# A wide Toeplitz table loaded in eight bands of 16 partitions in place of four bands of 32

## What is computed

```python
# layer 0: linear attention over the normalised image, then a layer norm
x = x + _L0_conv_ref(_gn(x), L0_conv_w_qkv, ...)
# layer 1: 7 x 7 depthwise circular convolutions, by FFT in the reference
gate_A = sigmoid(conv(x, gate_A_kernel)); gate_B = sigmoid(conv(x, gate_B_kernel))
b_t = conv(x, B_kernel) * gate_B
# 8 equal steps of a gated scan, then h_final @ W_out + b_out
x = x + _L1_conv_ref(_gn(x), ...)
```

## Time and profile before

| | before |
|---|---|
| median of 3 runs | 6455.65 us (6454.68 to 6463.24) |
| the profiled execution | 6477.81 us, span 6476.0 us |
| busy: TensorE matmul, weight load | 87%, 80% |
| busy: VectorE, ScalarE, GpSimd | 66%, 61%, 65% |
| moved by DMA | 1440.33 MB, mean 222 GB/s |
| granted TensorE clock, mean | 0.953 |

### The profile page before, as it was taken

How to read it: one execution, slowest core, us unless ns; L and a number is a source line. 1 busy time by engine, 2 the same in 40 slices (tenths; PEclk the granted TensorE clock), 3 DMA queues, 4 the chain that set the end, 5 groups by cost and what they waited for, 6 DMA issues and landing times. The chain is left out here.

```text
span 6476.0 us, 143235 instructions
## 1 busy us (share of the span) xinstructions
PE 5612.8 (87%) x51252; PEld 5161.6 (80%) x51252; DVE 4301.7 (66%) x5123; ACT 3942.8 (61%) x5128; POOL 4179.6 (65%) x3608
## 2 busy tenths in 40 slices
PE   6789999999999999999972688888888888888887
PEld 5578888888888888888862578887878778888887
DVE  6367667776667676677745976666666667666653
ACT  5677677776677666677522456565555555565554
POOL 0146666666666666676674977767667677677651
PEclk9899999999999999999986799999999999999999
DMA  5457777777777777777664599999999999999987
GB/s 129 130 158 224 218 221 224 224 218 217 219 222 221 222 218 218 217 226 222 183 175 131 150 252 257 266 260 261 254 251 256 251 260 262 254 266 260 251 239 211
DMA packets 1239217, 1440.33 MB, mean 222 GB/s; under 512 B 142960, under 2 KB 1025396, under 8 KB 1238516
## 3 DMA queue, kind: packets, MB, share of 16 engines
q1 hardware_dynamic: 1238516, 1431.07, 77.8%
HBM read 999.09 MB, written 431.64 MB: 221 GB/s over the span
## 5 line engine op out<-in xcount | busy, mean ns | idle before, releaser
L1231 PE MATMUL psC<-wide,xhl 128*128 128x256 bf16 x6144 | 1058.0, 283 | 58.1 <-DMA wide<-toeplitz_wide 47.3
L1228 PE MATMUL psC<-wide,xhl 128*128 128x192 bf16 x6144 | 877.6, 253 | 0.0
L1161 POOL TENSOR_TENSOR stage<-stage,nrow 128x1024 f32<-128x1024 f32 x240 | 622.4, 2593 | 365.6 <-DMA stage<-x_by_block_row 354.4
L787 POOL TENSOR_TENSOR y<-y,grow 128x1024 f32<-128x1024 f32 x256 | 606.1, 2367 | 344.1 <-DVE y L654 344.1
L1178 POOL COPY down<-xhl 48x448 f32<-48x448 f32 x512 | 505.8, 988 | 490.9 <-PE psC L1237 387.2
L1322 ACT ACTIVATE xhl<-psC 128x512 f32<-128x512 f32 x512 | 303.3, 599 | 694.5 <-PE psC L1237 693.0
L1237 PE MATMUL psC<-narrow,down 128*128 128x96 bf16 x6144 | 540.3, 213 | 162.2 <-POOL down L1181 95.8
L1228 PEld LDWEIGHTS psC<-wide,xhl 128*128 128x128 bf16 x6144 | 646.8, 116 | 20.2
L1231 PEld LDWEIGHTS psC<-wide,xhl 128*128 128x128 bf16 x6144 | 598.3, 116 | 73.5 <-DMA wide<-toeplitz_wide 47.1
L1429 DVE SCALAR_TENSOR_TENSOR xhl<-xhl,psC 128x512 f32<-128x512 f32 x512 | 346.6, 680 | 466.6 <-ACT xhl L1322 466.1
L1337 ACT ACTIVATE hT<-psH 128x512 f32<-128x512 f32 x512 | 304.8, 595 | 539.3 <-PE psH L1273 539.0
(11 more groups left out here) (167 smaller groups left out, 13803.6 us busy)
## 6 DMA issues: line engine op xcount, KB each, us to landing
wide<-toeplitz_wide SPq DMA_DIRECT2D x1024, 140.0 KB, 5.8
xa<-in_x SPq DMA_DIRECT2D x256, 512.0 KB, 4.5
xb<-in_x SPq DMA_DIRECT2D x256, 512.0 KB, 3.6
xc<-in_x SPq DMA_DIRECT2D x256, 512.0 KB, 5.8
x_rows<-xc SPq DMA_DIRECT2D x256, 512.0 KB
res<-x_rows SPq DMA_DIRECT2D x256, 512.0 KB, 8.7
out<-res SPq DMA_DIRECT2D x256, 512.0 KB, 8.0
stage<-x_by_block_row SPq DMA_DIRECT2D x225, 512.0 KB, 8.4
```

Of the source, the lines that this page charges most:

```text
L787: nc.gpsimd.tensor_tensor(y[:], y[:], grow[:].unsqueeze(1).to_broadcast([P, TPC, C]), ALU.mult).then_inc(s_yg, 1)
L1161: nc.gpsimd.tensor_tensor(v, v, nrow[:, 0:1, :].to_broadcast([P, NP_, C]), ALU.mult).then_inc(s_scaled, 1)
L1228: nc.tensor.matmul(dst[:, :, :, 2:], lhs, tab[:, :, 32 + part * 12:44 + part * 12], start=False, stop=False)
L1231: nc.tensor.matmul(dst, lhs, tab[:, :, part * 16:part * 16 + 16], start=(n == 0), stop=False)
```

## The change

A second list of ranges, `LOADS`, has eight bands for groups of 16 partitions: rows 0 to 2, 0 to 4, 0 to 6, 0 to 8, 2 to 10, 4 to 12, 6 to 14 and 8 to 16. `load_wide` issues eight DMAs by it in place of four, and TensorE's wait counts 16 for each of them. Setup goes on storing by `BANDS`. Ring depths and the order of everything else stay.

```diff
 BANDS = [(max(0, 4 * g - 6), 4 * g + 4) for g in range(4)]
+LOADS = [(max(0, 2 * g - 6), 2 * g + 2) for g in range(8)]
...
-                for g in (0, 2, 1, 3):
-                    lo, hi = BANDS[g]
-                    rows = slice(g * 32, (g + 1) * 32)
+                for g in (0, 4, 2, 6, 1, 5, 3, 7):
+                    lo, hi = LOADS[g]
+                    rows = slice(g * 16, (g + 1) * 16)
                     sp.dma_start(wide[rows, blk % WR, lo:hi].rearrange("p r c e -> p (r c e)"),
                                  wide_d[blk, rows, lo * CB * WCOL:hi * CB * WCOL]).then_inc(s_w[blk % WR], 16)
...
-                pe.wait_ge(s_w[k], img * (64 * uses(NBLK, WR, k)) + 64 * (blk // WR + 1))
+                pe.wait_ge(s_w[k], img * (16 * len(LOADS) * uses(NBLK, WR, k)) + 16 * len(LOADS) * (blk // WR + 1))
```

## The result

The changed kernel takes 6976.95 us (median of 4 runs, 6969.61 to 6987.72), the kernel before beside it 6459.44 us (6454.68 to 6470.68). The ratio is 1.0804, 95% interval 1.0782 to 1.0826: slower by 8%, 517 us. The forecast was slower by 2.5%, 6615 us, and at most 6790. The profiled execution took 6987.72 us, its span 6985.9.

A forecast was written before the change was run, and what follows sets the result against it. The SP queue issuing every DMA was to become the bound: 14 images x (9.1 + 2.5) = 162 us on 6477.8 or the 6455.65 median, giving 6640 or 6618; forecast 6615 us, +2.5%, range 6420 to 6790.

The forecast's parts named there:

- 128 x 0.466 = 59.6 us per image: SP queue, second layer: four more wide-load DMAs per block, 128 per image, each priced at 0.466 us.
- The slot of 0.466 us: SP queue: one wide load's price, its median issue of 0.421 us plus a gap of 0.045 us.
- the high end of the slot (0.53 us): SP queue: estimated upper average price of one wide load with stalls in it, 67.8 us per image.
- at least 4.1: End of an image, SP already full: blocks spaced 3.47 us between narrow loads go to at least 4.1 us.
- a twentieth of the old waits: SP queue, steady images: 2.5 us per image added for imperfect packing, out of 50.5 us of waits.
- I take nothing for the bytes: Wide table, 84 KB less per block: possible gain of 0 to 7.9 us per image, counted as nothing.
- Faster by shorter issues: SP's wide loop: issues of 0.35 us leave SP waits, lighter DMA cuts table waits; 6400 or 6345 us; chance 0.17.
- DMA engines: Wide-table transfers: 16 partitions may be written more slowly; at half of today's rate 6800 us; chance 0.12.
- threshold of 11.9 GB/s: Wide table per DMA engine: 364 KB fit the remaining 1.96 us per block only above this rate, 70% of 17.0.
- SP's waits for blocks: Sign on the SP queue: waits for finished blocks fall from 599 us to under a tenth of the period.
- the median issue: Sign on the SP queue: a wide load's median issue time stays at 0.42 us.
- the image at 188 us: Sign in the second layer: the steady image takes about 188 us, against 176.8 us before.

The follow-up runs named there:

- the run made for it: Kernel before with its four wide loads covering 16 partitions and all 16 rows each, same bytes and number of issues: 6783.96 us, ratio 1.0492.

## Why the prediction was wrong, point by point

**The mechanism was right; SP's added work was priced too low.** That SP becomes the bound is shown three ways: it waits 0.7 us per image for blocks; the time moves by at most 0.5% with the bytes (1.0804, 1.0789 and 1.0751 with 364, 448 and 56 KB); and it goes with the number of its issues, 6459 us at four, 6977 at eight, 7895 at twelve. The step that failed is "128 x 0.466 = 59.6 us per image": it adds slots at their median and leaves all other issues at their old price. The added work measured 84.6 us.

**The account.** Per image SP went from 126.3 to 210.9 us of work, where 185.9 was forecast, and from 50.5 to 0.7 us of waits, where I allowed 2.5. The pieces:

- The slot of 0.466 us, times 128: 59.6 us. Right; the median issue is 420 ns, eight in a row take 3.65 us, and from eight issues to twelve the image grows by 60.1 us.
- The narrow load's median issue went from 0.320 to 0.522 us, 32 x 0.202 = 6.5 us. I had left it at its old price. The row of before that could have warned me is the narrow load at 4432.44, issued in 0.52 us right behind a store. In the kernel before its median is 0.52 us within 0.15 us behind a store or a stage load and 0.32 us when the queue had paused for over 0.7 us; right behind a wide load it is 0.35 us (0.36 in the changed kernel). So 0.32 us was the price behind a pause, and the changed queue has hardly any.
- The issues of over 1 us rose from 10.3 to 30.0 us per image above the medians of their kinds: 19.7 us. I had seen them and put them in the high end of the slot (0.53 us) but not in the forecast. Neither value was the right form: they are no part of an added wide load's price, since twelve issues have no more of them than eight. They come where the queue loses its pauses, above all behind stores and residual loads. At the end of an image I even left them out of a row that showed them: the 3.47 us between two narrow loads hold 1.2 us of them, and with four more slots make 5.3 us, not "at least 4.1"; in the changed kernel they follow each other after 5.5 us at the median where only wide loads stand between.
- Together 59.6 + 6.5 + 19.7 = 85.8 us, 1.2 us more than the 84.6 measured; that rest is not assigned.
- The waits left, 0.7 in place of 2.5 us: 1.8 us too many. I had taken a twentieth of the old waits, a number with no row behind it. SP never caught up except a few times.

6.5 + 19.7 - 1.2 - 1.8 = 23.2 us per image, and 188.4 + 23.2 = 211.6. Over the 14 images of the sum that is 325 us. A further some 20 us came in after image 14, which I had put at nothing: what follows image 13 grew by 53.9 us, 34.8 of them image 14's if it lost as much as those before it.

**"I take nothing for the bytes"** was right: at four issues they are worth 27 us, at eight nothing.

**The rivals.** *Faster by shorter issues*: an issue of 16 partitions costs what one of 32 costs; the rows of the same line were the right ones to go by. *DMA engines*: narrow transfers do lower the rate of all traffic, by 11% in the run made for it (17.0 to 15.1 GB/s per engine). The rival's threshold of 11.9 GB/s is for the wide table alone. With the prediction's 3.56 us per block for all other traffic, an estimate, the table ran at about 12 GB/s in that run (28 KB per engine in 0.98 x 6.06 - 3.56 = 2.38 us), so the rival was nearer than the 11% say. In the changed kernel it ran at about 14 (22.75 KB in 0.79 x 6.61 - 3.56 = 1.66 us), which fits into the old period, and the engines have 21% of their time free. By the run with four loads of 16 the Trainium skill's rule (SBUF — State Buffer, "Door 1: The DMA port swizzle") holds in its direction, though the table's rate fell by some 30% where the ports halve. Its other sentence (DMA: Bandwidth & Descriptors, "Issuing engines are not separate DMA queues"), that the time to start a DMA is usually small relative to the DMA, does not fit this kernel, where the starts are the whole loss.

**The signs named ahead** came out as follows: SP's waits for blocks at 0.7 us of 211.6 per image, or 4% by the view of waits (right either way); eight loads in 3.68 us (3.65, but not all); the median issue (right); the image at 188 us (211.6); the DMA share near 0.84 (0.79, as the image is longer); TensorE's table waits above 103 us with sooner landings (525.2 us; right).

**What stays open** is why an issue behind a 512 KB store or load takes 1.2 to 2.4 us when the queue does not pause. It does so with 56 KB and with 448 KB per block in the wide table, with 16 and with 32 partitions. No run changed the 512 KB transfers or their place.

## What to carry to other kernels

Count the time of the queue that issues the DMAs like that of an engine: waits per period, times slots, against the waits that it has left. Take the price of every issue on it, old and new, from stretches in which the queue is full, with the same transfer in front, and add up the long ones; medians and stretches behind a pause leave them out. Check a queue's waits against what it waits for: a line of waits can hold time that the queue spent issuing. Put what must arrive first ahead of the bulk, or on another queue. A DMA share of 95% is no proof that bytes are worth an issue: cut the bytes alone once, at the same number of transfers, and see.

## What the runs showed that was not expected

- An issue costs 0.42 us at the median whether it moves 7 KB (one row, 16 partitions) or 140 KB, and each issue added to a full queue makes the image 0.469 us longer.
- What an issue costs depends on what stands before it. The narrow load, the same 168 KB, takes 0.32 us behind a pause, 0.35 us right behind a wide load and 0.52 us right behind a store; the wide load after that narrow one takes 2.05 us at the median in the changed kernel.
- At 95% busy, the DMA engines could lose seven eighths of the wide table's bytes for a gain of 0.6%.
- TensorE's granted clock went from 0.96 (four issues) to 0.91 (eight) and 0.85 (twelve) as it waited more, and its matmuls for the same work took 1940, 2086 and 2313 us in 13 images. It is hardly a part of the loss: a faster TensorE could have shortened the steady image only by what SP waited for it, 0.7 us at eight issues and nothing at twelve.
